# Turning the byte panels of the count matrix on ScalarE and VectorE together

## The reference

```python
def gcn_conv(h, W, b, src, dst, num_nodes):          # three times
    h = h @ W
    ...
    msg = h[src] * norm[:, None]
    agg = jax.ops.segment_sum(msg, dst, num_segments=num_nodes)
...
agg = jax.ops.segment_sum(x[src], dst, num_segments=num_nodes)   # SAGE
```

## Time and profile before

| | |
|---|---|
| median of 3 runs | 11630.27 us (11602.31 to 11649.21) |
| the profiled execution | 11612.36 us, its span 11610.4 us |
| granted TensorE clock, mean | 0.796 |
| busy: PE, DVE, ACT, POOL | 67%, 41%, 35%, 58% of the span |
| the four sum passes | about 7990 to 11540 us |

### The profile page before, as it was taken

The page is one execution under the profiler, slowest core; times in us unless marked ns, Lnnn a source line. Parts: engine busy times, 40 slices in busy tenths (PEclk is TensorE's granted clock), DMA queues, the critical chain, the costliest instruction groups (busy, mean ns, idle before and its releaser), DMA issues. The chain is left out here.

```text
span 11610.4 us, 188078 instructions
## 1 busy us (share of the span) xinstructions
PE 7835.2 (67%) x44374; PEld 6657.0 (57%) x44375; DVE 4722.3 (41%) x11571; ACT 4065.0 (35%) x5411; POOL 6777.7 (58%) x6167
## 2 busy tenths in 40 slices
PE   4777777787887736666666776675665665564566
PEld 3777777777777725555555555554454454453445
DVE  5544444444444464444444443334222222224223
ACT  0000000000000022333333333333774774775676
POOL 3566666566655457777676666664553554453553
PEclk8888888888888767777777778886887887887788
DMA  7211111111111122222222222223564554554554
GB/s 267 98 14 14 14 14 13 13 14 13 13 13 11 7 48 60 60 58 59 57 58 55 54 56 56 55 55 77 140 153 108 137 151 108 137 146 121 130 139 111
DMA packets 808282, 843.70 MB, mean 73 GB/s; under 512 B 313245, under 2 KB 602316, under 8 KB 808139
## 3 DMA queue, kind: packets, MB, share of 16 engines
q1 hardware_dynamic: 285755, 569.75, 16.2%
q0 software_dynamic: 519824, 272.11, 15.6%
q10 hardware_dynamic: 2560, 0.53, 0.0%
HBM read 718.90 MB, written 123.02 MB: 73 GB/s over the span
## 5 line engine op out<-in xcount | busy, mean ns | idle before, releaser
L850 PE MATMUL psAB<-one_hot,arena 128*128 128x128 f32 x15680 | 2499.0, 321 | 678.3 <-issue 389.2
L574 POOL DMA_INDIRECT gath<-sum_tab,idx_block x1792 | 1789.0, 998 | 1811.2 <-DVEq L1123 925.4
L850 PEld LDWEIGHTS psAB<-one_hot,arena 128*128 128x128 f32 x15680 | 2303.4, 224 | 768.7 <-issue 711.2
L574 POOL DMA_INDIRECT gath<-spline_tab,idx_block x1568 | 1508.2, 962 | 1421.9 <-DVEq L1123 912.7
L548 POOL DMA_INDIRECT dense<-count_block,cell_block x1120 | 1880.3, 1679 | 492.1 <-issue 338.7
L973 PE MATMUL psCD<-arena_r 128*128 128x512 f32 x5096 | 1600.7, 468 | 730.5 <-ACT arena_r L759 526.5
L574 POOL DMA_INDIRECT gath<-gat_tab,idx_block x1568 | 1562.7, 997 | 908.8 <-DVEq L1123 450.8
L973 PEld LDWEIGHTS psCD<-arena_r 128*128 128x128 f32 x5096 | 1109.0, 229 | 1098.7 <-issue 869.4
L1446 DVE SCALAR_TENSOR_TENSOR one_hot<-iota_row,tile_base,dstf 128x512 fp32r<-128x512 f32 x632 | 476.2, 754 | 2258.9 <-PE psAB L959 1371.6
L690 ACT ACTIVATE edge_count<-psE x490 | 83.9, 171 | 3538.1 <-remote 2367.5
L1184 DVE TENSOR_SCALAR one_hot<-iota_row,tile_base,dstf 128x128 fp32r<-128x128 f32 x1952 | 614.4, 357 | 1205.0 <-remote 794.7
(11 more groups left out here) (262 smaller groups left out, 10723.9 us busy)
## 6 DMA issues: line engine op xcount, KB each, us to landing
arena<-dst_rows SPq DMA_DIRECT2D x392, 256.0 KB
stage<-dense SPq DMA_DIRECT2D x208, 448.0 KB
hT<-dense SPq DMA_DIRECT2D x208, 448.0 KB
arena<-dense SPq DMA_DIRECT2D x208, 448.0 KB
dense<-stage SPq DMA_DIRECT2D x91, 896.0 KB
early<-dense SPq DMA_DIRECT2D x104, 448.0 KB
gath<-sum_tab,idx_block POOLq DMA_INDIRECT x1792
gath<-spline_tab,idx_block POOLq DMA_INDIRECT x1568
```

The costliest lines, as they stand in the source:

```text
L574: nc.gpsimd.indirect_dma_start(out=dest[:, s, j, :], out_offset=None, in_=table, in_offset=bass.IndirectOffsetOnAxis(ap=idx_block[:, c:c + ...
L850: nc.tensor.matmul(block, z[:, w, j, k * P:(k + 1) * P], oh32[:, j, :], start=(j == 0), stop=(j == J - 1))
```

## The change

ScalarE converts the first five tiles' counts of each panel (AT = 5 * QC = 2560 columns), VectorE the last two (1024 columns, `turn_part`), both into the same `counts[w]`. `panel_turned[w]` is raised by each of them, so SP and PE wait for twice the count. VectorE converts the two units ahead of group s + 1 after it has finished group s of the sparse part; those of units 0 and 1 of a stretch come after group 7 of the stretch before (for the first stretch, after the 8 groups ahead of it). Each waits for `panel_used` and `panel_loaded` as ScalarE does. The last stretch stands apart from the loop, as it has no units to convert for a next one.

```diff
--- before.py
+++ after.py
@@ -69,7 +69,8 @@
     UC = UB * QC
     NP = 7
     CAP = 120
-    LEAD = 4
+    LEAD = 8
+    AT = 5 * QC
     SI = ID + 1
     QI = 1
     LI = SI + NQ * QI
@@ -485,12 +486,12 @@
 
                 with sp.Fori(0, NQ) as q:
                     for u in range(NU):
-                        sp.reg_add(need, turned, (u + NP) // 2 + 1 + LEAD - NP)
+                        sp.reg_add(need, turned, 2 * ((u + NP) // 2 + 1 - NP) + LEAD)
                         sp.wait_ge(loaded_edges, 16 * 9)
                         sp.wait_ge(panel_turned[(u + 1) % 2], need)
                         sp.dma_start(panel[u % NP].unsqueeze(1),
                                      dense_rows[:, bass.ds(q, 1), u * UC:(u + 1) * UC]).then_inc(panel_loaded[u % NP], 16)
-                    sp.reg_add(turned, turned, NP)
+                    sp.reg_add(turned, turned, 2 * NP)
 
             sp.wait_ge(dense_known, 1)
             sp.wait_ge(scattered, 16 + 16 * DP)
@@ -756,7 +757,7 @@
                         act.wait_ge(loaded_edges, 16 * 9)
                         act.wait_ge(panel_used[w], free)
                         act.wait_ge(panel_loaded[b], loaded)
-                        nc.scalar.activation(counts[w], panel[b], ACT.Copy).then_inc(panel_turned[w], 1)
+                        nc.scalar.activation(counts[w][:, 0:AT], panel[b][:, 0:AT], ACT.Copy).then_inc(panel_turned[w], 1)
                     act.reg_add(used, used, NU // 2)
                     act.reg_add(folded, folded, 1)
                     act.wait_ge(loaded_edges, 16 * 9)
@@ -964,7 +965,7 @@
             def dense_unit(u):
                 w = u % 2
                 if w == 0:
-                    pe.reg_add(turned, turned, 1)
+                    pe.reg_add(turned, turned, 2)
                 pe.wait_ge(loaded_edges, 16 * 9)
                 if u == 0:
                     pe.wait_ge(piece_split, pieces)
@@ -1433,7 +1434,21 @@
             for r in ends:
                 dve.reg_mov(r, SV - 1)
 
-            def sum_groups(i):
+            loaded, free = registers(dve, "dve_panel", 2)
+
+            def turn_part(u):
+
+                w, b = u % 2, u % NP
+                if b == 0:
+                    dve.reg_add(loaded, loaded, 16)
+                if w == 0:
+                    dve.reg_add(free, free, 1)
+                dve.wait_ge(loaded_edges, 16 * 9)
+                dve.wait_ge(panel_used[w], free)
+                dve.wait_ge(panel_loaded[b], loaded)
+                V.tensor_copy(counts[w][:, AT:UC], panel[b][:, AT:UC]).then_inc(panel_turned[w], 1)
+
+            def sum_groups(i, turning=False, again=True):
                 group_bounds(dve, i, regs)
                 for s in range(S):
                     col = i * (S * J) + s * J
@@ -1452,6 +1467,9 @@
                         add_sum(visit, SV - 1)
                     shift(dve, ends, need)
                     give_back(s)
+                    if turning:
+                        for u in units_before((s + 1) % S) if again or s + 1 < S else ():
+                            turn_part(u)
 
             def add_dense(q):
 
@@ -1472,10 +1490,13 @@
                     dve.reg_mov(r, 0)
                 with dve.Fori(first, SI) as i:
                     sum_groups(i)
-                with dve.Fori(0, NQ) as q:
-                    for w in range(QI):
-                        sum_groups(q * QI + (SI + w))
+                for u in units_before(0):
+                    turn_part(u)
+                with dve.Fori(0, NQ - 1) as q:
+                    sum_groups(q + SI, turning=True)
                     add_dense(q)
+                sum_groups(LI - 1, turning=True, again=False)
+                add_dense(NQ - 1)
                 for k in range(SV - 1):
                     dve.reg_add(late, visit, k + 1)
                     add_sum(late, SV - 2 - k)
```

## The result

The changed kernel takes 11570.1 us in the median of 20 runs, the kernel before 11622.4 us in 20 runs on the same chip: a ratio of 0.9956, 95% interval 0.9944 to 0.9968. It is faster by 0.44%, where 1.1% was forecast: the direction was right, the size less than half. The profiled execution has a span of 11543.3 us against 11610.4. "Stretch" is used as in the prediction: one of 13 pieces of a sum pass.

The account below looks back on a forecast made before the run. ScalarE's conversions bound undisturbed pieces, late TensorE signals during POOL's long gather rows the rest. Terms -283 + 119 + 3 + 30 = -131 us gave 11481, plus 18 for the median: 11500 us; own range 11400 to 11600, with rivals 11320 to 11740.

Parts of the forecast that it names:

- Part (1): ScalarE's conversion shrinks from 3584 to 2560 elements, 0.854 us less; 332 TensorE waits for it shorten: -283 us.
- A reading ahead of it: Old trace: TensorE's unit ends at 8318.21, ScalarE waits for that buffer, next unit starts 8330.80 after 9.52 us idle.
- Part (2): VectorE gets 728 copies of 128x1024, 0.80 us each beside POOL, lying beside TensorE's work; up to 9.5 us on POOL.
- Rival A: VectorE's copy runs at one element a cycle, 1.35 us: 11640 us, no change; chance 0.20.
- Part (3): VectorE's new wait on panel_used: after two-visit groups TensorE's next unit starts 0.92 us later, 129 times: +119 us.
- Part (4): What moves: panel loads wait for both engines, nothing; copies ahead of each pass's first stretch, +3 us; last stretch, nothing.
- Part (5): More late TensorE signals, as POOL's share of a stretch rises and copies lengthen gathers: +30 us, the least certain term.
- rival C: POOL never rests: longer gather rows, more late signals, TensorE and VectorE both waiting on them; 11730 us, chance 0.25.
- the forecast's own counter-sign: Forecast is wrong if TensorE comes to wait for one-hot builds more than for converted panels.
- its other one: Forecast is wrong if TensorE's waits for the two converting engines together do not fall under 400 us.
- Rival B: VectorE tied to TensorE's units returns gather slots singly, breaking long gather rows; half of 310 us goes: 11320, chance 0.10.
- The cause read into the earlier trace: While POOL issues some ten or more gathers unbroken, TensorE's signals come 4 us and more late, in most stretches.

Follow-up runs that it names:

- act_five: Kernel before with ScalarE converting five of seven tiles and nobody the other two: ratio 1.001 on a chip with late signals, 0.9684 (again) on one without.
- after_again: The changed kernel itself, unaltered, rerun on a chip without late signals: ratio 0.991 to the kernel before.
- copy_first: Changed kernel with each visit's reduce and add moved ahead of the next one-hot, the last visit's behind the copies: 0.9754 without late signals, 0.9849 with them.
- lockstep_again: Changed kernel with ScalarE converting all seven tiles and VectorE only waiting and signalling, on a chip without late signals: ratio 1.0119 to the kernel before.
- before_again: The kernel before, unaltered, rerun for a profile on a chip without late signals: ratio 0.9992.

## Why the prediction was right in kind and wrong in size

- *Part (1), -283 us.* Right where signals are prompt: act_five_again gains 307 us, and PE's waits for ACT fall by 289 there. On a late chip the same edit gains nothing (1.001), and why is open. The sum took a saving in PE's list of waits for time. A reading ahead of it is wrong as well: between the unit that ends at 8318.21 and the one at 8330.80, called the next unit, lies another one, at 8319.43 us; the late signal itself is real.
- *Part (2).* Right: 0.697 us for the copy, in the sum 0.68 to 0.80. Rival A is out. POOL did not lose the up to 9.5 us a stretch beside the copies: the mean gather went from 998 to 1022 ns, 0.8 us for the 32 gathers of a stretch.
- *Part (3), +119 us, is the step that failed: it priced the stall and put what the stall does to the matmuls behind it at nothing.* The stall itself was priced right: 2.49 us against a forecast 2.4 in the group shown, and on the chip of the result 0.68 us more in the mean of 156 groups, 106 us. (The forecast took 129 groups at 0.92; three in a stretch stand before a pair of units, 156.) What was left out is that PE, having rested twice, often goes on at 1.2 GHz: the matmuls behind these groups take 5.02 us in place of 4.45 on the chip of the result, 0.57 x 156 = 89 us, which is more than the 64 us that lie between the forecast -131 and the -67 of the span. On prompt chips VectorE's share of the work costs (0.991 - 0.9684) x 9732 = 220 us in all, the difference of after_again and act_five_again. PE's records have it as 300.7 - 210.9 = 90 us more idle time before the units and 1529.3 - 1405.6 = 124 us more of unit matmuls. copy_first, which takes the stall away, gets 1.6 of these 2.3% back, PE's idle time and its busy time shrinking by 101 us each. How the 220 us split between the waits' place and the copies' length was not measured on a prompt chip. The prediction had seen a half-clock pair behind a long wait, and gave that price to late signals alone.
- *Part (4).* Nothing read in the runs speaks against it; ACT's listed wait for a load was 53.2 us and is 52.3.
- *Part (5), +30 us, looks too small as well on late chips.* The share of late signals rose from 13 to 18%, and the waits for one-hots by 156 us, while unlabelled waits before the units and waits for gathers fell by 185. I read the rise as rival C's mechanism at part of its price: a late signal holds VectorE, and behind it the builds that PE needs next. No run tests this reading. On the chip of the result the forecast's own counter-sign came true: PE waits longer for one-hots (518.1 us) than for turned panels (379.1), while its other one did not (379.1 is under 400).
- *Rival B* is out: gathers came in rows as before (58 rows of twelve or more in the sum passes, 62 before), and late signals became more frequent, not rarer.
- The cause read into the earlier trace rows, that POOL's unbroken rows of gathers make PE's signals late, was never put to the test, since the runs made for it fell on prompt chips. On late chips the two go together, as counted above, which does not say which brings the other, or whether a third thing brings both. On prompt chips rows as long delay nothing, so they are not enough by themselves.

On prompt chips the change gives -307 + 220 = about -87 us; next to the sum that is 24 us more of gain, no late signals (30 less) and 98 us more for the waits. On the chip of the result the direction, -52 us between the medians, is right partly by luck: the only gain in the sum is part (1), and it was worth nothing when it ran alone on another late chip. The changed kernel and act_five were not measured side by side on any chip.

## What to carry to other kernels

When work moves to an engine that other work already hangs on, price the stall it makes on TensorE together with the matmuls behind it: on the prompt chips 0.83 us of extra rest ahead of the 156 pairs of units went with 0.81 us more in the 14 matmuls of each (after_again against act_five_again). Then look at what stands ahead of the moved work in its queue; with two small operations put behind it instead of before it, the change was worth 2.5% instead of 0.8% on the same chip. And a saving read from a list of waits need not come as time: act_five's was worth 3.2% on one kind of chip and nothing on the other. Run the saving alone, without its price, before building the whole.

## What the runs showed of the hardware that was not expected

- The same kernel takes 9.73 ms on three chips and 11.18 to 11.62 ms on the others. On the slower ones 13 to 22% of TensorE's recorded signals arrive over 2.5 us after the instruction's end, some of them 10 us and more, nearly all while POOL is in a row of gathers; on the faster ones at most 0.1% do, beside rows as long.
- A kernel can lose 1.2% with the same idle time before its units, by the granted clock: in lockstep_again PE is busy 1975 us for the work that took 1880.
- Two rests of about a microsecond, 1.25 and 0.85 us in the median, go before a lowered clock in 71% of the pairs of units behind two-visit groups (after_again); where the second one is not there, in 19% (before_again).
- VectorE's copy of 128x1024 from uint8 to fp32r takes 0.69 us in the median and 0.95 at most, and the mean gather is longer beside such copies: 1039 ns in after_again, 997 in before_again. It cost nothing that a run could show there: the change is worth as much with half the gathers (0.990).
